# L1-distance attention scores in a vision tower: tiles 9/5/2 over VectorE, GpSimd and TensorE in place of 11/5

## The chip, the cores and the metric

One core of one Trainium2 chip runs the whole kernel in one launch. The metric is the device time of that launch in microseconds (us), lower is better. Before the change it is 2816.99 us, the median of 3 runs.

## The reference, cut to what matters

A tower runs over 128 images of 64 tokens with 64 features: wavelet tokeniser, linear attention, a mixture of experts, then the L1-distance attention that is changed here, and a routed MLP. The stage that matters:

```
q, vf, vb = split(x @ wqv_w.T + wqv_b)            # 8 heads of width w = 64 each
k = x[:, :, None, :] * wk
a[b,s,t,h] = -sum_w |q[b,s,h,w] - k[b,t,h,w]| / sqrt(64)
a = softmax over s, with one more row of zeros
o = (sum_s a[b,s,d,h] vf[b,s,h,:] + sum_s a[b,d,s,h] vb[b,s,h,:]) summed over h
y = (o * sigmoid(1.702 o)) @ fanin_w.T + fanin_b
```

For each image there are 64 x 64 x 8 = 32,768 sums of 64 absolute differences, 2.1 million differences. That is the bulk of the stage.

## The kernel before, in words

The stage loops over 64 pairs of images. Keys and queries are split into two f16 parts each. The DMAs of `fill_blocks` lay them out in `blocks`, so that one f16 matmul with a 0/1/-1 matrix `pick` makes a bank of 512 differences for each of 128 partitions: the partition is a (query, key) pair out of 128, and the column is (head, w). A tile is two such matmuls, into two banks of PSUM, 128 x 1024 differences. An image has 16 tiles.

The string `ORDER` gives the order of the 16 tiles on TensorE's in-order queue and says who sums each one:

- D: VectorE reads the tile from PSUM and sums absolute values over w in one instruction (`reduce`, L1337). Banks 0 to 3 hold two such tiles in turn, so TensorE may be two D tiles ahead of VectorE, and waits for semaphore `red` otherwise.
- A: ScalarE takes absolute values into SBUF (`absolute`, L977), and GpSimd adds the five A tiles of an image up in a tree of halvings (`batch`, L1452, and L1456 for the last step). Banks 4 and 5 hold one A tile, so TensorE waits for `abs` of the tile before. The SBUF tiles `absd0` and `absd1` alternate from image to image.

Before, ORDER has 11 D and 5 A. The work that surrounds the scores is hung between the tiles: `extra(b, k)` issues it on TensorE after tile k of image b of a pair. These are the projections of the next pair (`turn` L662, `queries` L668, `keys` L672), the values of the last (`values_b` L679, `values_f` L686), the attention sums of the pair before (`turn_attn` L694, `attend` L710 and L715) and the end of the one before that (`turn_y` L721, `fan_in` L725). On ScalarE the same is written out by hand in `pair` (L1007 to L1036): copies out of PSUM, the split of q and k (L956, L960), and eight exponentials in two parts (L989) sit between the calls of `absolute`. VectorE's `pair` (L1341) puts the low parts of q and k (`low`, L1316), `reciprocals`, `finish` and `gated` between its reduces. GpSimd has `normalise` (L1463) between two batches. The queue of SyncE issues 16 DMAs of `fill_blocks` (L388), 16 of `spread` (L397) and one load for each pair.

Of the kernel before, what the change touches and what calls it, by code (L numbers as in the profile page):

```python
# [22 lines left out]
D = 64  # L23
# [11 lines left out]

ORDER = "DADDADDADDADDADD"
ND, NA = ORDER.count("D"), ORDER.count("A")
W_SCALE = 64.0
# [71 lines left out]
def build(nc, a, out, scratch):  # L110

    with ExitStack() as ctx:
# [3 lines left out]
        def sem(name):  # L116
# [12 lines left out]
        c_rows = sb("c_rows_sb", [P, 64])  # L129
        c_cols = sb("c_cols_sb", [7, 2, 8, P])  # L130
        tok_w = sb("tok_w", [7, D])
# [13 lines left out]

        absd0 = sb("absd0", [P, NA * 1024])
        kT = absd0[:, 2048:3072].rearrange("p (b a m) -> p b a m", b=2, a=4)
        qT = absd0[:, 3072:3584]
# [95 lines left out]

        absd = [t[:].rearrange("p (n w) -> p n w", w=D) for t in (absd0, absd1)]
        wk_b = big[0:D, 0:QK].rearrange("p (h d) -> p h d", d=D)
# [18 lines left out]
            "xs", "wk_in", "consts", "xT_ps", "xT_sb", "xTq", "q_ps", "k_ps", "half", "tb0", "tb1",  # L265
            "diffD", "diffA", "red", "abs", "tree", "pooled", "spread0", "spread1", "exp", "zr", "attk", "attq_ps", "attq",
            "o_ps", "tanh", "y", "yT_ps", "yT", "fan_ps", "hx", "sum", "vb_ps", "vb", "vf_ps", "vf")}
# [53 lines left out]
        def _(sp):  # L321
# [114 lines left out]
        def _(pe):  # L436
# [220 lines left out]
            def turn(p, at):  # L657

                if at >= 3:
                    pe.wait_ge(X["sum"], p - 3)  # L660
                pe.wait_ge(X["xs"], 16 * (p + 1))
                pe.transpose(ps[7][:, 0:P], xs1[:], ident[:]).then_inc(X["xT_ps"], 1)  # L662
# [60 lines left out]
            def fan_in(p):  # L723
                pe.wait_ge(X["yT"], p + 1)
                pe.matmul(ps[7][:, 192:256], yT[:], fan[:], start=True, stop=True).then_inc(X["fan_ps"], 1)  # L725

            def image(q, b, at, extra):

# [3 lines left out]
                for k, path in enumerate(ORDER):  # L732
                    if path == "D":
                        if not (at == 0 and b == 0 and d < 2):
                            pe.wait_ge(X["red"], ND * s + d - 1)
                        unit, bank, done = 2 * d, 2 * ((b + d) % 2), "diffD"
                        d += 1
                    else:
                        if not (at == 0 and b == 0 and u == 0):
                            pe.wait_ge(X["abs"], NA * s + u)  # L740
                        unit, bank, done = 2 * (ND + u), 4, "diffA"
                        u += 1
                    for n in range(2):
                        mm = pe.matmul(ps[bank + n], pick[:, unit % 8 + n, :], blocks[:, b, unit // 16, unit // 8 % 2, :],  # L744
# [4 lines left out]
            def pair(q, odd, at):  # L749
                def extra(b, k):  # L750
                    if b == 0:
# [6 lines left out]
                        if k == 4 and at >= 3:  # L758
                            fan_in(q - 3)
                        if k == 7:  # L760
                            turn(q + 1, at)
                        if k == 9:
                            queries(q + 1, at)
                        if k == 14:
                            keys(q + 1, 1 - odd)
                    else:
                        if at >= 2:
                            if k == 4:
                                turn_attn(q - 2)
                            if 7 <= k < 10:  # L770
                                attend(q - 2, odd, k - 7)

# [14 lines left out]
            values_f(last, 1)  # L787
            fan_in(last - 2)
            for p, odd in ((last - 1, 0), (last, 1)):
                pe.wait_ge(X["attk"], p + 1)  # L790
# [45 lines left out]
        def _(act):  # L836
            act.dma_start(c_cols[:].rearrange("p a b c -> p (a b c)"), a["c_cols"]).then_inc(tok_in, 16)
            act.dma_start(tok_w[:], a["L0_tok_W"]).then_inc(tok_in, 16)
# [133 lines left out]
            def absolute(s, odd, u, first):  # L972

                act.wait_ge(X["diffA"], NA * s + u + 1)
                if u == 0 and not first:
                    act.wait_ge(X["pooled"], s - 1)
                nc.scalar.activation(absd[odd][:, 16 * u:16 * u + 16, :], pp[:, 4:6, :].rearrange("p n (h w) -> p (n h) w", w=D),  # L977
                                     ACT.Abs).then_inc(X["abs"], 1)

# [27 lines left out]
            def pair(q, odd, at):  # L1007
# [7 lines left out]
                if at >= 1:  # L1015
                    values_f(q - 1, 1 - odd)
                absolute(s, 0, 2, first)
                prepare_x(q + 1, 1 - odd)
                absolute(s, 0, 3, first)
                high_q(q + 1, False)  # L1020
                absolute(s, 0, 4, first)
                s += 1
                high_k(q + 1)
                absolute(s, 1, 0, first)
                absolute(s, 1, 1, first)
                if at >= 2:
                    turned_attn(q - 2)
                absolute(s, 1, 2, first)
                absolute(s, 1, 3, first)
                if at >= 2:  # L1030
                    gate_o(q - 2)
                if at >= 1:
                    exponentials(q - 1, 0, at == 1)
                absolute(s, 1, 4, first)
                if at >= 1:
                    exponentials(q - 1, 1, at == 1)  # L1036

            act.wait_ge(pads, PADS)
# [10 lines left out]
            turned_y(last - 2)  # L1049
            values_f(last, 1)  # L1050
            for p in (last - 1, last):
                turned_attn(p)
# [23 lines left out]
        def _(dve):  # L1076
# [10 lines left out]
            for t in (xT4[D:D + 1, :], xT1[D:D + 1], xTq[D:D + 1, :], yT[D:D + 1, :]):  # L1087
                dve.memset(t, 1.0).then_inc(pads, 1)
            dve.memset(wk_bd[:], 0.0)
            dve.memset(wqv_bd[:], 0.0)  # L1090
# [243 lines left out]
            def reduce(s, odd, b, d):  # L1334
                dve.wait_ge(X["diffD"], ND * s + d + 1)
                bank = 2 * ((b + d) % 2)
                dve.tensor_reduce(score[:, odd, b, 16 * d:16 * d + 16],  # L1337
# [3 lines left out]
            def pair(q, odd, slot, at):  # L1341
                for b in range(2):
# [3 lines left out]
                    for d in range(ND):  # L1346
                        reduce(2 * q + b, odd, b, d)
                        if b == 0 and d == 0 and at >= 2:
                            reciprocals(q - 2)
                        if b == 0 and d == 4 and at >= 3:  # L1350
                            finish(q - 3, slot)
                        if b == 0 and d == 8:
                            low(q + 1, 0)
                        if b == 1 and d == 1:
                            low(q + 1, 1)
                        if b == 1 and d == 8 and at >= 2:
                            gated(q - 2)
# [49 lines left out]
        def _(pool):  # L1407
# [37 lines left out]
            def batch(s, p, odd, b, at):  # L1445

                x = absd[b]
                pool.wait_ge(X["abs"], NA * (s + 1))
                for m, w in enumerate((32, 16, 8, 4, 2)):
# [4 lines left out]
                if at >= 2:  # L1454
                    pool.wait_ge(X[f"spread{b}"], 16 * 8 * (p - 1))
                nc.gpsimd.tensor_tensor(score[:, odd, b, 16 * ND:256].unsqueeze(2), x[:, :, 0:1], x[:, :, 1:2],  # L1456
                                        ALU.add).then_inc(X["pooled"], 1)
# [64 lines left out]
```

## Time and profile before

| what | value |
|---|---|
| runs | 2816.99 us median (2815.43 to 2818.05) |
| profiled execution | 2817.37 us, its span 2815.6 us |
| busy | VectorE 82%, TensorE 76%, GpSimd 62%, ScalarE 49% of the span |
| the attention stage | from about 700 to 2620 us of the span; granted TensorE clock 1.00 in it |

Busy time of TensorE counts each matmul until its last result is written, so neighbours overlap. A line of the timeline gives the start, the length, the engine, the source line, the operation, its output and inputs and how many instructions are merged; in brackets is the idle time of the engine before it and what ended that. Times of TensorE's weight loads stand apart, as PEld.

### The profile page before, as it was taken

To read this page: it belongs to the slowest core of one execution; us is meant where nothing else is said; L and a number is where in the kernel's file an instruction comes from. 1 tells how busy PE (TensorE), PEld (TensorE's weight loads), DVE (VectorE), ACT (ScalarE), POOL (GpSimd) and SP (SyncE) were. 2 spreads that over 40 slices of the span, in tenths; PEclk is the share of its full clock that TensorE was granted. 3 is DMA by queue.
4 is the path that set the end of the run, shared out by engine and by line. 5 is a ranking of instruction groups with operands and counts; after the bars stand their busy time and mean duration, and the time that the engine had idled before them with its cause. 6 is when DMAs were issued, how large, how long until landed. Compare 5 with 4: busy or idle time off the path is not lost.

```text
span 2815.6 us, 43219 instructions
## 1 busy us (share of the span) xinstructions
PE 2145.3 (76%) x11861; PEld 898.4 (32%) x11861; DVE 2322.0 (82%) x2847; ACT 1380.3 (49%) x2997; POOL 1750.9 (62%) x1015
## 2 busy tenths in 40 slices
PE   4649999994777777777777777777777777777466
PEld 3533333331223223223223323223222232232245
DVE  3877778788889889889899899899899899898542
ACT  0325555552455555555555555555555555555234
POOL 0103333232588888887887887887887887887411
PEclk8879999997899999999999999999999999999768
DMA  5100000000111111111111111111111111111000
GB/s 136 44 1 1 1 0 0 0 0 2 49 44 47 46 41 46 47 42 45 47 43 43 47 45 43 47 46 43 45 47 43 44 47 44 43 47 46 16 11 19
DMA packets 163208, 101.96 MB, mean 36 GB/s; under 512 B 55773, under 2 KB 161182, under 8 KB 163039
## 3 DMA queue, kind: packets, MB, share of 16 engines
q1 hardware_dynamic: 162858, 101.41, 14.6%
q8 instruction: 17, 0.28, 0.0%
q10 hardware_dynamic: 316, 0.12, 0.0%
q14 instruction: 17, 0.14, 0.0%
HBM read 10.63 MB, written 4.19 MB: 5 GB/s over the span
## 4 chain that ended last, share of the span: by engine, by line
PE 47%; DVE 29%; issue 16%; ACT 3%; DVEq 2%; DMA 1%; SPq 1%; POOL 1%; ACTq 0%; POOLq 0%
DVE score L1337 21%; PE pp L744 14%; PE pp L593 5%; DVE qk L1316 3%; PE pp L715 3%; PE pp L686 2%; PE pp L614 2%; PE pp L672 2%; PE pp L618 2%; PE pp L615 2%; PE pp L619 2%; PE pp L679 2%; PE pp L585 1%; PE pp L710 1%; ACT vb L966 1%
## 5 line engine op out<-in xcount | busy, mean ns | idle before, releaser
L1337 DVE TENSOR_REDUCE score<-pp 128x16 f32<-128x1024 f32 x1408 | 1644.1, 1217 | 192.5 <-PE pp L744 189.4
L1452 POOL TENSOR_TENSOR absd<-absd 128x2560 f32<-128x2560 f32 (+4 forms) x640 | 1450.1, 2266 | 368.0 <-ACT absd L977 327.9
L744 PE MATMUL pp<-blocks,pick 128*128 128x512 f16 x4096 | 1111.6, 382 | 199.5 <-DVE score L1337 161.8
L977 ACT ACTIVATE absd<-pp 128x1024 f32<-128x1024 f32 x640 | 655.0, 1023 | 712.7 <-PE pp L744 712.7
L744 PEld LDWEIGHTS pp<-blocks,pick 128*128 128x128 f16 x4096 | 316.2, 98 | 852.3 <-DVE score L1337 464.1
L1428 POOL TENSOR_TENSOR absd<-absd,yw 128x512 f32<-128x512 f32 x112 | 142.3, 1270 | 318.9 <-DVE yw L1255 318.9
L916 ACT ACTIVATE absd<-pp 128x512 f32<-128x512 f32 x256 | 150.8, 596 | 148.2 <-PE pp L615 145.7
L1271 DVE SCALAR_TENSOR_TENSOR absd<-pp,absd 128x512 f32<-128x512 f32 x256 | 172.4, 687 | 53.2 <-ACT absd L916 38.6
L989 ACT ACTIVATE expd<-attn 128x65 f32<-128x65 f32 x512 | 155.6, 315 | 0.0
L593 PE MATMUL pp<-absd 128*64 128x512 f32 x512 | 138.1, 618 | 0.0
L672 PE MATMUL pp<-wk_diag,xT 96*128 96x512 f32 x130 | 74.1, 652 | 73.0 <-DVE qk L1316 73.0
L662 PE MATMUL pp<-ident,xs 128*128 128x128 f32 x65 | 21.0, 323 | 128.8 <-DVE h L1332 93.7
L686 PE MATMUL pp<-wqv,xT 96*64 96x256 f32 x512 | 69.4, 392 | 44.3 <-ACT vb L966 44.3
L989 ACT ACTIVATION_READ_ACCUMULATOR expd<-attn 128x1 f32 x512 | 100.9, 197 | 0.0
L960 ACT ACTIVATE qk<-pp 128x512 f16<-128x512 f32 x65 | 38.8, 597 | 125.6 <-PE pp L672 125.6
L614 PE MATMUL pp<-x,absd 128*128 128x512 f16 x256 | 98.4, 384 | 0.8
L618 PE MATMUL pp<-x,absd 128*128 128x512 f16 x256 | 97.8, 382 | 0.3
L619 PE MATMUL pp<-x,absd 128*128 128x512 f16 x256 | 97.5, 381 | 0.0
L615 PE MATMUL pp<-x,absd 128*128 128x512 f16 x256 | 97.5, 381 | 0.0
L1316 DVE SCALAR_TENSOR_TENSOR qk<-qk,pp 128x512 f16<-128x512 f16 x130 | 88.0, 677 | 6.9 <-ACT qk L956 4.1
L1255 DVE TENSOR_TENSOR yw<-pp,absd 128x512 f32<-128x512 f32 x112 | 77.1, 688 | 17.8 <-PE pp L593 15.3
L920 ACT COPY absd<-pp 128x512 f32<-128x512 f32 x128 | 75.0, 586 | 27.7 <-PE pp L585 18.8
(200 smaller groups left out, 2201.8 us busy)
## 6 DMA issues: line engine op xcount, KB each, us to landing
blocks<-qk SPq DMA_DIRECT2D x1032, 64.0 KB, 2.0
attn<-score SPq DMA_DIRECT2D x1024, 16.0 KB, 1.8
xs<-xn SPq DMA_DIRECT2D x66, 32.0 KB, 1.8
big<-in_wrb_t SPq DMA_DIRECT2D x1, 2064.0 KB
big<-in_x_rows SPq DMA_DIRECT2D x4, 512.0 KB, 6.2
token_rows<-big SPq DMA_DIRECT2D x8, 256.0 KB, 2.0
big<-in_L_ffn_w SPq DMA_DIRECT2D x4, 512.0 KB, 10.0
out<-big SPq DMA_DIRECT2D x16, 128.0 KB, 2.0
```

The source lines that it names most:

```text
L593: mm = pe.matmul(ps[4 + k % 2][64 * e:64 * e + 64, :], w3[:, 2 * k + e, :], hid[:, 2 * (k % 2) + e, :], start=True, stop=True)
L614: pe.matmul(ps[e], w12_hi[:, 0, 2 * k + e, :], x2[:, b, :], start=True, stop=False)
L615: pe.matmul(ps[e], w12_lo[:, 0, 2 * k + e, :], x2[:, b, :], start=False, stop=True).then_inc(C["h1_ps"], 1)
L618: pe.matmul(ps[2 + e], w12_hi[:, 1, 2 * k + e, :], x2[:, b, :], start=True, stop=False)
L619: pe.matmul(ps[2 + e], w12_lo[:, 1, 2 * k + e, :], x2[:, b, :], start=False, stop=True).then_inc(C["h2_ps"], 1)
L744: mm = pe.matmul(ps[bank + n], pick[:, unit % 8 + n, :], blocks[:, b, unit // 16, unit // 8 % 2, :], start=True, stop=True)
L977: nc.scalar.activation(absd[odd][:, 16 * u:16 * u + 16, :], pp[:, 4:6, :].rearrange("p n (h w) -> p (n h) w", w=D), ACT.Abs).then_inc(X["a ...
L989: op = nc.scalar.activation(expd[:, n, :], attn[:, :, n], ACT.Exp, scale=-(float(D) ** -0.5), accum_out=zst[:, 0, n:n + 1])
L1271: dve.scalar_tensor_tensor(out=hid[:, 2 * (k % 2) + e, :], in0=ps[2 + e], scalar=1.0 / W_SCALE, in1=silu[:, e, :], op0=ALU.mult, op1=ALU.m ...
L1316: dve.scalar_tensor_tensor(out=qk[:, kind, 1, :], in0=qk[:, kind, 0, :], scalar=-LO_SCALE, in1=ps[6], op0=ALU.mult, op1=ALU.add).then_inc( ...
L1337: dve.tensor_reduce(score[:, odd, b, 16 * d:16 * d + 16], pp[:, bank:bank + 2, :].rearrange("p n (h w) -> p (n h) w", w=D), AX.X, ALU.add, ...
L1452: nc.gpsimd.tensor_tensor(x[:, :, 0:w], x[:, :, 0:w], x[:, :, w:2 * w], ALU.add).then_inc(X["tree"], 1)
```

## The change

ORDER becomes `DADDADADADDADEDE`: 9 D tiles, 5 A tiles, and 2 tiles of a new kind E. For an E tile the operands of the matmul change places: a slice of `blocks` of 128 columns is the stationary operand and `pick` is the moving one. So a bank has (two heads, w) over its 128 partitions and 512 (query, key) pairs over its columns. ScalarE takes absolute values into `abse`, a part of the same SBUF tiles, and TensorE sums over the partitions: `sum_e` uses each 128 x 128 slice of `abse` as stationary operand against `pair_ones`, two columns of ones for the two heads, all in f32. That is 16 such matmuls an image, in four groups g of four, and 32 columns of PSUM bank 7 as result, which ScalarE copies into `score` (`take_e`).

A and E tiles are now handed over by halves of 512 columns: `diffA` and `abs` count halves, and `absolute` issues two activations for each tile, so that banks 4 and 5 are used as two buffers. The items between the tiles move to other places in ORDER. `fill_blocks` waits for `diffA` in place of `diffD`, and `spread` waits for `etaken` too. The diff, cut:

```diff
-ORDER = "DADDADDADDADDADD"
-ND, NA = ORDER.count("D"), ORDER.count("A")
+ORDER = "DADDADADADDADEDE"
+ND, NP, NE = ORDER.count("D"), ORDER.count("A"), ORDER.count("E")
+NA = NP + NE
...
+        pair_ones = sb("pair_ones", [P, 2])
...
+        abse = [t[:, NP * 1024:NA * 1024].rearrange("p (m n) -> p m n", m=4) for t in (absd0, absd1)]
...
             def fill_blocks(p, b, first):
                 if not first:
-                    sp.wait_ge(X["diffD"], ND * (2 * (p - 1) + b + 1))
+                    sp.wait_ge(X["diffA"], 2 * NA * (2 * (p - 1) + b + 1))
...
             def spread(p, odd, b, first):
                 sp.wait_ge(X["pooled"], 2 * p + b + 1)
+                sp.wait_ge(X["etaken"], 2 * p + b + 1)
...
             def attend(p, odd, part):
                 if part == 0:
+                    pe.wait_ge(X["etaken"], 2 * p + 5)
...
+            def sum_e(s, b, g, first):
+                if g == 0:
+                    pe.wait_ge(X["abs"], 2 * NA * s + 2 * NA)
+                    if not first:
+                        pe.wait_ge(X["etaken"], s)
+                for m in range(4):
+                    mm = pe.matmul(ps[7][:, 384 + 8 * g + 2 * m:384 + 8 * g + 2 * m + 2], abse[b][:, m, P * g:P * g + P],
+                                   pair_ones[:], start=True, stop=True)
+                if g == 3:
+                    mm.then_inc(X["e_ps"], 1)
...
+                        for n in range(2):
+                            if not (at == 0 and b == 0 and u == 0):
+                                pe.wait_ge(X["abs"], 2 * NA * s + 2 * u + n - 1)
+                            if path == "A":
+                                unit = 2 * (ND + u) + n
+                                pe.matmul(ps[4 + n], pick[:, unit % 8, :], blocks[:, b, unit // 16, unit // 8 % 2, :],
+                                          start=True, stop=True).then_inc(X["diffA"], 1)
+                            else:
+                                m = 2 * (u - NP) + n
+                                pe.matmul(ps[4 + n], blocks[:, b, 1, 1, P * m:P * m + P],
+                                          pick[:, 4:8, :].rearrange("p a b -> p (a b)"), start=True, stop=True).then_inc(X["diffA"], 1)
...
-                        if k == 7:
+                        if k == 8:
                             turn(q + 1, at)
-                        if k == 9:
+                        if k == 10:
                             queries(q + 1, at)
-                        if k == 14:
+                        if 11 <= k < 15 and at >= 1:
+                            sum_e(2 * q - 1, 1, k - 11, False)
+                        if k == 15:
                             keys(q + 1, 1 - odd)
                     else:
+                        if 2 <= k < 6:
+                            sum_e(2 * q, 0, k - 2, at == 0)
                         if at >= 2:
-                            if k == 4:
+                            if k == 6:
                                 turn_attn(q - 2)
-                            if 7 <= k < 10:
-                                attend(q - 2, odd, k - 7)
+                            if 8 <= k < 11:
+                                attend(q - 2, odd, k - 8)
...
+            def take_e(s, p, odd, b, at):
+                act.wait_ge(X["e_ps"], s + 1)
+                if at >= 2:
+                    act.wait_ge(X[f"spread{b}"], 16 * 8 * (p - 1))
+                nc.scalar.copy(score[:, odd, b, 224:256], ps[7][:, 384:416]).then_inc(X["etaken"], 1)
```

The new order on ScalarE is, in image 0 of a pair: A0, values_b, turned_y, A1, values_f, A2, A3, prepare_x, A4, high_q, E5, take_e of the image before, E6; in image 1: high_k, A0, A1, take_e of image 0, A2, turned_attn, A3, A4, gate_o, exponentials part 0, E5, exponentials part 1, E6. On VectorE, `finish` follows reduce 3 (was 4) and `low` reduce 7 of image 0 and 2 of image 1 (were 8 and 1).

## Rows read from the trace of the kernel before

**Rows 1.** The page's head: span, and busy time of each engine.

```profile
span 2815.6 us, 43219 instructions
PE 2145.3 (76%) x11861; PEld 898.4 (32%) x11861; DVE 2322.0 (82%) x2847; ACT 1380.3 (49%) x2997; POOL 1750.9 (62%) x1015
```

**Rows 2.** Stretches: us, busy of PE, PEld, DVE, ACT, POOL, PEclk, DMA.

```profile
180.00:200.00 20.00, 1.87 (x8) 1.38 (x8) 16.51 (x11) 1.65 (x4) 0.80 (x2) 0.50 0.00 0
...
860.00:2605.00 1745.00, 1338.20 (x7795) 521.25 (x7793) 1569.84 (x1571) 925.12 (x2093) 1414.00 (x756) 1.00 0.18 45
...
2640.00:2660.00 20.00, 10.60 (x110) 8.29 (x110) 2.81 (x6) 5.85 (x23) 1.89 (x2) 0.50 0.03 7
```

**Rows 3.** Timeline of VectorE (DVE) in one pair.

```profile
2006.66 0.21 DVE L1332 TENSOR_TENSOR h<-pp,h 128x64 f32 x1
...
2007.80 4.62 DVE L1337 TENSOR_REDUCE score<-pp 128x16 f32<-128x1024 f32 x4 [0.93 <-PE pp L744]
2012.33 0.68 DVE L1316 SCALAR_TENSOR_TENSOR qk<-qk,pp 128x512 f16<-128x512 f16 x1
...
2036.67 0.21 DVE L1332 TENSOR_TENSOR h<-pp,h 128x64 f32 x1
```

**Rows 4.** Timeline of GpSimd (POOL) in the same pair.

```profile
2009.73 1.04 POOL L1463 TENSOR_TENSOR attk<-expd,zst 128x512 f32<-128x512 f32 x1
2012.38 11.66 POOL L1452 TENSOR_TENSOR absd<-absd 128x2560 f32<-128x2560 f32 x5 [1.61 <-ACT absd L977]
2024.21 0.32 POOL L1456 TENSOR_TENSOR score<-absd 128x80 f32<-128x80 f32 x1 [0.16 <-POOL absd L1452]
```

**Rows 5.** Timeline of TensorE (PE) in the same stretch.

```profile
2007.17 1.03 PE L744 MATMUL pp<-blocks,pick 128*128 128x512 f16 x4
2008.03 1.02 PE L668 MATMUL pp<-wqv,xTq 96*128 96x512 f32 x2
2008.89 1.03 PE L744 MATMUL pp<-blocks,pick 128*128 128x512 f16 x4
...
2018.80 0.66 PE L694 MATMUL pp<-ident,attk 128*128 128x128 f32 x4 [0.69 <-DVE qk L1316]
...
2032.13 1.08 PE L686 MATMUL pp<-wqv,xT 96*64 96x256 f32 x8 [0.70 <-ACT vb L966]
2033.15 0.60 PE L744 MATMUL pp<-blocks,pick 128*128 128x512 f16 x2
2033.59 0.33 PE L725 MATMUL pp<-fan,yT 96*128 96x64 f32 x2
2033.76 1.72 PE L744 MATMUL pp<-blocks,pick 128*128 128x512 f16 x6
```

**Rows 6.** The chain of work that ended last, in order of time.

```profile
2021.59 0.54 PE pp L744 x2
2022.12 0.61 PE pp L715 x16
```

**Rows 7.** Timeline of TensorE in the mixture of experts.

```profile
199.22 1.89 PE L565 MATMUL pp<-gate,xT 96*128 96x16 f32 x8 [0.67 <-ACT xT L900]
...
443.62 1.07 PE L565 MATMUL pp<-gate,xT 96*128 96x16 f32 x8
444.54 1.08 PE L603 MATMUL pp<-eye,absd 128*128 128x64 f32 x8
445.46 0.38 PE L614 MATMUL pp<-x,absd 128*128 128x512 f16 x1
```

**Rows 8.** Timeline of ScalarE (ACT) in the same pair.

```profile
2025.48 0.32 ACT L989 ACTIVATE expd<-attn 128x65 f32<-128x65 f32 x1
...
2026.69 1.02 ACT L977 ACTIVATE absd<-pp 128x1024 f32<-128x1024 f32 x1
...
2031.50 0.58 ACT L966 COPY vb<-pp 128x512 f32<-128x512 f32 x1
```

**Rows 9.** Groups by line, 900 to 2600 us: busy, mean ns; idle before.

```profile
L956 ACT ACTIVATE qk<-pp 128x512 f16<-128x512 f32 x57 | 33.7, 591 | 0.0
```

More of the change, by code:

```diff
@@ L146, in build @@
         absd0 = sb("absd0", [P, NA * 1024])
+        c_cols = absd0[0:7, 0:2048].rearrange("p (o c m) -> p o c m", o=2, c=8)
         kT = absd0[:, 2048:3072].rearrange("p (b a m) -> p b a m", b=2, a=4)
@@ L243, in build @@
         tok_rows = big[:].rearrange("p (u n) -> p u n", u=8)
-        absd = [t[:].rearrange("p (n w) -> p n w", w=D) for t in (absd0, absd1)]
+        absd = [t[:, 0:NP * 1024].rearrange("p (n w) -> p n w", w=D) for t in (absd0, absd1)]
+        abse = [t[:, NP * 1024:NA * 1024].rearrange("p (m n) -> p m n", m=4) for t in (absd0, absd1)]
         wk_b = big[0:D, 0:QK].rearrange("p (h d) -> p h d", d=D)
@@ L735, in image @@
                             pe.wait_ge(X["red"], ND * s + d - 1)
-                        unit, bank, done = 2 * d, 2 * ((b + d) % 2), "diffD"
+                        unit, bank, done = 2 * d, 2 * ((ND * b + d) % 2), "diffD"
                         d += 1
                     else:
-                        if not (at == 0 and b == 0 and u == 0):
-                            pe.wait_ge(X["abs"], NA * s + u)
-                        unit, bank, done = 2 * (ND + u), 4, "diffA"
+                        for n in range(2):
[9 more added lines that the diff above has]
+                                          pick[:, 4:8, :].rearrange("p a b -> p (a b)"), start=True, stop=True).then_inc(X["diffA"], 1)
                         u += 1
+                        extra(b, k)
+                        continue
                     for n in range(2):
@@ L788, in _ @@
             fan_in(last - 2)
+            pe.wait_ge(X["sum"], last - 1)
+            for g in range(4):
+                sum_e(2 * last + 1, 1, g, False)
+            pe.wait_ge(X["etaken"], 2 * PAIRS)
             for p, odd in ((last - 1, 0), (last, 1)):
@@ L836, in _ @@
         def _(act):
-            act.dma_start(c_cols[:].rearrange("p a b c -> p (a b c)"), a["c_cols"]).then_inc(tok_in, 16)
+            act.dma_start(c_cols.rearrange("p a b c -> p (a b c)"), a["c_cols"]).then_inc(tok_in, 16)
             act.dma_start(tok_w[:], a["L0_tok_W"]).then_inc(tok_in, 16)
@@ L972, in absolute @@
             def absolute(s, odd, u, first):
[L974 to L978, printed above, removed]
+                for n in range(2):
+                    act.wait_ge(X["diffA"], 2 * NA * s + 2 * u + n + 1)
+                    if u == 0 and n == 0 and not first:
+                        act.wait_ge(X["pooled"], s - 1)
+                    if u == NP and n == 0 and not first:
+                        act.wait_ge(X["e_ps"], s - 1)
+                    if u < NP:
+                        nc.scalar.activation(absd[odd][:, 16 * u + 8 * n:16 * u + 8 * n + 8, :],
+                                             ps[4 + n].rearrange("p (h w) -> p h w", w=D), ACT.Abs).then_inc(X["abs"], 1)
+                    else:
+                        nc.scalar.activation(abse[odd][:, 2 * (u - NP) + n, :], ps[4 + n], ACT.Abs).then_inc(X["abs"], 1)
+            def take_e(s, p, odd, b, at):
[3 more added lines that the diff above has]
+                nc.scalar.copy(score[:, odd, b, 224:256], ps[7][:, 384:416]).then_inc(X["etaken"], 1)
             def exponentials(p, part, first):
@@ L1017, in pair @@
                 absolute(s, 0, 2, first)
+                absolute(s, 0, 3, first)
                 prepare_x(q + 1, 1 - odd)
-                absolute(s, 0, 3, first)
+                absolute(s, 0, 4, first)
                 high_q(q + 1, False)
-                absolute(s, 0, 4, first)
+                absolute(s, 0, 5, first)
+                if at >= 1:
+                    take_e(s - 1, q - 1, 1 - odd, 1, at - 1)
+                absolute(s, 0, 6, first)
                 s += 1
@@ L1025, in pair @@
                 absolute(s, 1, 1, first)
+                take_e(s - 1, q, odd, 0, at)
+                absolute(s, 1, 2, first)
                 if at >= 2:
                     turned_attn(q - 2)
-                absolute(s, 1, 2, first)
                 absolute(s, 1, 3, first)
+                absolute(s, 1, 4, first)
                 if at >= 2:
@@ L1033, in pair @@
                     exponentials(q - 1, 0, at == 1)
-                absolute(s, 1, 4, first)
+                absolute(s, 1, 5, first)
                 if at >= 1:
                     exponentials(q - 1, 1, at == 1)
+                absolute(s, 1, 6, first)
             act.wait_ge(pads, PADS)
@@ L1050, in _ @@
             values_f(last, 1)
+            take_e(2 * last + 1, last, 1, 1, 4)
             for p in (last - 1, last):
@@ L1088, in _ @@
                 dve.memset(t, 1.0).then_inc(pads, 1)
+            for half in range(2):
+                for n in range(2):
+                    dve.memset(pair_ones[64 * half:64 * half + 64, n:n + 1], float(n == half))
             dve.memset(wk_bd[:], 0.0)
@@ L1349, in pair @@
                             reciprocals(q - 2)
[L1350 removed]
+                        if b == 0 and d == 3 and at >= 3:
                             finish(q - 3, slot)
[L1352 removed]
+                        if b == 0 and d == 7:
                             low(q + 1, 0)
[L1354 removed]
+                        if b == 1 and d == 2:
                             low(q + 1, 1)
[L1356 removed]
+                        if b == 1 and d == 7 and at >= 2:
                             gated(q - 2)
```

12 lines of the change are left out of this document (7 added, 5 removed).

## Prediction

> **What bounds the kernel now.** I read the page's head first, then the busy time by stretch, then one pair of images on each engine's timeline. VectorE is the busiest engine [rows 1]. In the attention stage it is busy 1569.84 of 1745 us, or 90%, against TensorE 77%, GpSimd 81% and ScalarE 53%, at a granted clock of 1.00 [rows 2]. The same instruction (`finish`) starts at 2006.66 and 2036.67, so a pair takes 30.01 us [rows 3]. Four reduces in a row take 4.62 us, 1.15 each. VectorE's own work in a pair is 22 x 1.15 + 2 x 0.6 (`low`, whose 0.68 overlaps its neighbour by 0.08) + 0.5 of small items = 27.0 us, and the other 3.0 us are waits for TensorE. So VectorE bounds the stage, with TensorE's in-order stream as the thing that it waits for. GpSimd needs, for a pair, two batches from 2012.38 to 2024.53 (12.15 us) and one 1.04 us = 25.3 us [rows 4].
>
> **TensorE's own work in a pair, now.** This must be known without its waits, from starts of neighbours [rows 5]. Four f16 matmuls of 512 columns go from 2007.17 to 2008.03: 0.215 each, 0.43 a tile, 32 tiles = 13.8. A 96 x 512 f32 projection goes from 2008.03 to 2008.89: 0.86, three of them = 2.6. `values_f` is 2032.13 to 2033.15 = 1.02; `fan_in` 2033.59 to 2033.76 = 0.17; `turn_attn` 0.66 less the drain of 0.17 = 0.49; `turn` and `turn_y` about 0.26 by the same reckoning. The three parts of `attend` cost (0.54 - 0.43) + 0.61 = 0.72 each [rows 6] = 2.2. The sum is 20.5 us of 30.
>
> **The change part by part.**
>
> VectorE loses 4 reduces a pair: 4 x 1.15 = 4.6, so it needs 22.4 us. GpSimd keeps 5 tiles and its 25.3 us. The tiles' own matmuls stay 64: an E tile streams 512 f16 columns as an A tile does.
>
> The sums of E are new. Each image has 16 f32 matmuls with 128 stationary columns and 2 moving ones. An f32 matmul shows as two instructions (`fan_in` is x2), so a group g of four is 8 instructions. The trace has nearly the same thing: eight with 128 stationary and 16 moving columns start at 443.62, the next eight with 64 moving ones at 444.54, and what follows at 445.46 [rows 7]. So a group costs 0.92 whether 16 or 64 columns stream, and 2 will not make it cheaper: the weight loads set it. `fan_in`, behind a long f16 matmul, took 0.17 for two, which suggests that the first load is hidden there. That bounds a group by 0.84 and 0.92; I take 0.88, nearest to both. Eight groups a pair are 7.0 us (6.7 to 7.4), and TensorE's own work becomes 27.5 us. That is above every other engine.
>
> The Trainium skill, "TensorE: Matmul & The Clock Gate", section "Part 2: What happens when you issue a matmul", says that the queue pulls the load of the next weights ahead, so that they load while this tile's matmul runs. If that hid these loads, a group would cost only the page's floor of about 25 ns a matmul (section "Back-to-back issue gap" calls it the issue floor), 0.2 us by an estimate from it, and the change would win. The equal 0.92 of 16 and 64 columns [rows 7] speaks against it: two columns are too short to hide a load behind.
>
> ScalarE's 10 tiles of 1.02 become 28 halves. A 512-column activation takes 0.59 [rows 9], 0.49 when the next overlaps it by 0.1, as the tile at 2026.69 and its neighbours do [rows 8]. Hence 13.7 for 9.2, plus 2 x 0.2 for `take_e`: about 21 us of work. That is not the bound, but TensorE can run just one tile of A or E ahead of it. Four exponentials take from 2025.48 to 2026.69 = 1.21 us [rows 8].
>
> Setup (four small memsets, the shared space of `c_cols`) I cost at nothing: the memsets are behind the wait for the first input, and if they were not, they would be under 1 us.
>
> SyncE issues 33 DMAs a pair as before. `spread` of the second image now waits for `take_e`, which runs in the next pair's image 0, and it lands some 6 us after image 1 begins. The exponentials come 12 us after. So this is hidden, with 6 us to spare. `fill_blocks` waits for the last E matmul, and the next image's start is 5 us or more behind its landing.
>
> **A walk through one pair.** I follow TensorE's queue with these costs. Latencies: 0.05 from ScalarE (2031.50 + 0.58 to 2032.13), the same from VectorE, 0.04 to ScalarE, a half's result 0.38 after its start (0.60 for a tile, less 0.215). Its waits for ScalarE:
> - Image 0, k1: the halves of E6 of the image before are behind the second exponentials: 0.2 + 0.3.
> - k3: `values_f` waits for the copy of `vb`, which is queued behind A0: 0.4.
> - k6: A2 waits for A1, whose halves ScalarE clears every 0.49 while TensorE makes one in 0.215: 0.3. k8, with the copy of `vf` in between: 0.6. `queries` behind `prepare_x`: 0.2.
> - Image 1: `attend` waits for the copy of the turned attention: 0.3. k13 (E5) waits for A4: 0.5. k15 (E6) waits for E5, which on ScalarE stands behind four exponentials of 1.21: 1.2 + 0.3.
>
> They sum to 2.0 and 2.2. Image 0 has 14.4 us of work (16 tiles 6.9, three projections 2.6, `values_f` 1.0, four groups 3.5, small items 0.4) and takes 16.4; image 1 has 13.0 (6.9, 3.5, `turn_attn` 0.5, `attend` 2.1) and takes 15.1. The period is 31.5 us against 30.0. VectorE is never late in it: the banks of D tiles are always free, since TensorE takes 31.5/18 = 1.75 us for each D. GpSimd has both absd tiles in time, because batch s - 2 ends before A0 of image s.
>
> 62 pairs in the steady state x 1.54 = 95 us. At the end of the stage the last batch of GpSimd starts with A4 at tile 11, not 13, which hides the last sums; I leave it at 0. On the profiled 2817.37 us this gives 2912; the median of runs, 2816.99, is as good as the same, and I predict **2912 us**. What a measurement here can tell from no change is about 0.2%, or 6 us.
>
> **Rivals.**
>
> - *Faster: the waits vanish.* TensorE has 27.5 us of work, so if less than 2.5 us of waits remain it wins. With 1.3 us of waits the period is 28.8: 2817 - 62 x 1.2 = 2743. For it: VectorE, who made TensorE wait in the old order, is out of the way. Against: six of the waits are ScalarE clearing two halves at 0.49, and do not depend on VectorE. It decides at 2.5 us. 10%.
> - *Faster: the loads are hidden*, by the page's rule. A group of 8 then costs about 0.3, as 16 instructions of 64 stationary columns take 0.61 [rows 6]; 8 x 0.58 = 4.6 us less, period 27: 2817 - 185 = 2632. It decides at 0.69 a group. [rows 7] say 0.92. 3%.
> - *The change does what it says*, VectorE's 4.6 us in full: 25.4, GpSimd's floor, 2532. It would need TensorE's stream to fit in 25.4, and it does not. Under 1%.
> - *No change:* the period comes out within 0.1 us of 30.0. Only by accident: 3%.
> - *Slower still: the clock.* Between the four groups TensorE streams only 0.43 us of every 1.31. In [rows 2] the clock stood at 0.50 for 2640 to 2660 though TensorE was busy 10.6 of 20 us with small f32 matmuls; the attention stage itself held 1.00 with `attend` in it. If the clock fell from 2.4 to 1.2 GHz for both stretches of groups, a group costs 1.89 (the eight at 199.22, at a clock of 0.50 [rows 2, 7]) and a tile 0.86: 4 x (1.01 + 0.43) = 5.8 us a stretch, 11.5 a pair, up to 3620 us. The skill's same page, "A second HAM failure mode: psum-queue depth-cycling", warns that short idles between groups of matmuls can make the clock oscillate. Only a part of the stretches seems possible to me. 6%.
> - *Slower by more waits:* each new handover on TensorE costs a little that my walk leaves out. This is in the likeliest case's range.
>
> **How the numbers follow.** The likeliest case has 78%. Its own range: a group at 0.84 or 0.92 moves the period by -0.3 or +0.3, the waits by a quarter of 4.2 either way, so 30.2 to 32.9, or 2829 to 2995. I set the low end at 2830, the high end at 2995. Below lie about 13% in the faster cases and above the clock's 6%. Faster by over 0.2% 14%, within 3%, slower 83%.
>
> **What would show it.** After the change VectorE's share falls to about 70% in the stage and TensorE's rises to 90% or over. The distance of two `finish` is 31.5. The `sum_e` groups take 0.84 to 0.92 each, 7 us a pair. TensorE's largest waits are for `absolute` on ScalarE, the longest, over 1 us, before the E6 tile of image 1. GpSimd idles 5 to 6 us a pair. The prediction is wrong if a group costs under 0.7, if TensorE waits less than 2.5 us a pair, or if the clock leaves 1.00.

## The result, and the profile after

The changed kernel takes 2975.19 us (median of 4 runs), the kernel before 2817.52 us on the same chip. The ratio is 1.056, with a 95% interval of 1.054 to 1.058: 158 us slower. The forecast was 2912 us with 2830 to 2995 us as range. The trace shown is of the execution of 2975.75 us. The string ORDER above has two tiles the wrong way round: the changed kernel and all its variants run `DADADDADADDADEDE`, with the second A as tile 3 and not 4. The counts are the same.

First the page's head: span, busy times, and the granted clock in 40 slices.

```profile
span 2974.0 us, 54804 instructions
...
PE 2594.0 (87%) x15957; PEld 1437.0 (48%) x15957; DVE 2063.8 (69%) x2595; ACT 1692.5 (57%) x4277; POOL 1754.2 (59%) x1015
...
PEclk8879999996899999999999999999999999999768
```

Beside [rows 1], VectorE falls from 82% to 69% and TensorE rises from 76% to 87%. The busiest engine has changed. Next the stretches, read as [rows 2]:

```profile
760.00:900.00 140.00, 129.22 (x782) 74.63 (x781) 95.75 (x95) 86.80 (x227) 102.12 (x57) 0.92 0.18 42
900.00:2700.00 1800.00, 1653.33 (x10998) 954.63 (x10998) 1276.46 (x1280) 1155.70 (x3121) 1350.04 (x719) 0.97 0.17 42
```

In the attention stage TensorE is busy 92% of the time, VectorE 71%, ScalarE 64%, GpSimd 75%. The clock is 0.97 where it was 1.00, a small figure that will matter. VectorE's timeline gives the length of pairs, as in [rows 3]; `gated` is issued once a pair:

```profile
2007.88 0.21 DVE L1393 SCALAR_TENSOR_TENSOR osb<-osb,pp 128x64 f32<-128x64 f32 x1
...
2041.22 0.21 DVE L1393 SCALAR_TENSOR_TENSOR osb<-osb,pp 128x64 f32<-128x64 f32 x1
...
2072.71 0.21 DVE L1393 SCALAR_TENSOR_TENSOR osb<-osb,pp 128x64 f32<-128x64 f32 x1
```

The pairs are not alike: one takes 33.34 us, the next 31.49. The mean is 32.42 against 30.01 before. TensorE's timeline shows where they part. In the first pair, image 0, tile 14 and on:

```profile
2023.05 0.95 PE L745 MATMUL pp<-pair_ones,absd 128*128 128x2 f32 x8
2023.86 0.59 PE L778 MATMUL pp<-blocks,pick 128*128 128x512 f16 x2
2024.29 1.05 PE L745 MATMUL pp<-pair_ones,absd 128*128 128x2 f32 x8
2025.20 1.01 PE L772 MATMUL pp<-pick,blocks 128*128 128x512 f16 x2
2026.01 1.91 PE L680 MATMUL pp<-wk_diag,xT 96*128 96x512 f32 x2
2027.71 0.94 PE L778 MATMUL pp<-blocks,pick 128*128 128x512 f16 x2
```

and the same place one pair later, with the E6 tile of image 1:

```profile
2057.45 0.95 PE L745 MATMUL pp<-pair_ones,absd 128*128 128x2 f32 x8
2058.26 0.59 PE L772 MATMUL pp<-pick,blocks 128*128 128x512 f16 x2
2058.69 1.02 PE L680 MATMUL pp<-wk_diag,xT 96*128 96x512 f32 x2
2059.55 0.59 PE L778 MATMUL pp<-blocks,pick 128*128 128x512 f16 x2
...
2073.86 0.88 PE L772 MATMUL pp<-pick,blocks 128*128 128x512 f16 x2 [0.97 <-ACT absd L1026]
```

The E tile, the key projection and the next D tile take 0.81, 1.70 and 0.78 us from start to start in the first, 0.43, 0.86 and 0.43 in the second. The stretches say why:

```profile
2025.00:2028.00 3.00, 3.00 (x8) 1.28 (x8) 0.71 (x1) 1.32 (x4) 2.92 (x2) 0.50 0.05 11
2056.00:2059.00 3.00, 3.00 (x23) 2.56 (x22) 2.21 (x3) 1.60 (x4) 3.00 (x1) 1.00 0.00 0
```

The clock stood at 0.50 in one, 1.00 in the other, 1.2 and 2.4 GHz, and TensorE was recorded busy all of the time in both. In both it had just worked through four groups of sums without a gap. Among these each 1.24 us (2023.05 to 2024.29) holds one tile, 0.43 us of columns, and eight matmuls of two columns each, which are nearly all weight load. Why the clock falls in one pair of two and not in the other is not shown.

The drop is not the whole of the 1.85 us between the two pairs. From start to start, the last group, the E tile, the projection and the D tile take 0.91 + 0.81 + 1.70 + 0.78 = 4.20 us in the first and 0.81 + 0.43 + 0.86 + 0.43 = 2.53 in the second: the drop costs 1.67 us. The other 0.18 us is no clock: in wide_ones below, at a clock of 1.00, the pairs still alternate, with `gated` at 1987.74, 2019.87, 2051.81 and 2083.95, which is 32.13, 31.94 and 32.14. The likely place is the loop's end, as the kernel's loop holds two pairs: the D tile behind it starts 1.07 us after the tile before (2009.02 to 2010.09), for 0.71 inside the loop (2042.37 to 2043.08), and the profile names no engine that it waited for.

### The profile page after: what moved, and what is told of

It reads as the page before. It is cut to its first block, busy times and chain, and to the rows that moved or that the text cites. A ratio compares the mean times of both kernels' runs of the same rounds, so it can differ in the third digit from the quotient of the medians.

```text
span 2974.0 us, 54804 instructions
## 1 busy us (share of the span) xinstructions
PE 2594.0 (87%) x15957; PEld 1437.0 (48%) x15957; DVE 2063.8 (69%) x2595; ACT 1692.5 (57%) x4277; POOL 1754.2 (59%) x1015
## 4 chain that ended last, share of the span: by engine, by line
PE 64%; ACT 12%; DVE 10%; issue 10%; DVEq 2%; DMA 1%; ACTq 0%; POOL 0%; SPq 0%; POOLq 0%
PE pp L745 14%; PE pp L778 12%; DVE score L1403 5%; PE pp L768 5%; PE pp L599 4%; ACT expd L1044 3%; ACT absd L1026 3%; PE pp L680 3%; PE pp L772 3%; PE pp L725 3%; PE pp L694 2%; PE pp L620 2%; PE pp L676 2%; PE pp L624 2%; ACT absd L1023 2%
## 5 line engine op out<-in xcount | busy, mean ns | idle before, releaser
L1403 DVE TENSOR_REDUCE score<-pp 128x16 f32<-128x1024 f32 x1152 | 1380.7, 1222 | 605.8 <-PE pp L778 525.0
L1023 ACT ACTIVATE absd<-pp 128x512 f32<-128x512 f32 x1280 | 696.3, 598 | 414.8 <-PE pp L768 408.9
L745 PEld LDWEIGHTS pp<-pair_ones,absd 128*128 128x128 f32 x4096 | 544.2, 194 | 75.7 <-issue 0.7
L745 PE MATMUL pp<-pair_ones,absd 128*128 128x2 f32 x4096 | 493.5, 243 | 0.3 <-DVE h L1398 0.3
L778 PEld LDWEIGHTS pp<-blocks,pick 128*128 128x128 f16 x2304 | 199.9, 110 | 261.7 <-DVE score L1403 125.1
L1026 ACT ACTIVATE absd<-pp 128x512 f32<-128x512 f32 x512 | 278.2, 600 | 64.3 <-PE pp L772 62.6
L772 PE MATMUL pp<-pick,blocks 128*128 128x512 f16 x512 | 188.3, 410 | 78.2 <-ACT absd L1026 62.9
L768 PEld LDWEIGHTS pp<-blocks,pick 128*128 128x128 f16 x1280 | 122.8, 107 | 253.3 <-ACT absd L1023 91.7
L958 ACT ACTIVATE absd<-pp 128x512 f32<-128x512 f32 x256 | 150.8, 596 | 148.0 <-PE pp L621 143.4
L1033 ACT COPY score<-pp 128x32 f32<-128x32 f32 x128 | 23.8, 186 | 244.0 <-PE pp L745 244.0
L772 PEld LDWEIGHTS pp<-pick,blocks 128*128 128x128 f16 x512 | 54.0, 123 | 179.5 <-ACT absd L1026 120.1
L1044 ACT ACTIVATION_READ_ACCUMULATOR expd<-attn 128x1 f32 x512 | 108.0, 211 | 0.0
L620 PE MATMUL pp<-x,absd 128*128 128x512 f16 x256 | 98.4, 384 | 0.6
L624 PE MATMUL pp<-x,absd 128*128 128x512 f16 x256 | 97.8, 382 | 1.0 <-DVE absd L1337 0.3
L625 PE MATMUL pp<-x,absd 128*128 128x512 f16 x256 | 97.5, 381 | 0.0
```

The source lines that it names most:

```text
L620: pe.matmul(ps[e], w12_hi[:, 0, 2 * k + e, :], x2[:, b, :], start=True, stop=False)
L745: mm = pe.matmul(ps[7][:, 384 + 8 * g + 2 * m:384 + 8 * g + 2 * m + 2], abse[b][:, m, P * g:P * g + P], pair_ones[:], start=True, stop=True)
L768: pe.matmul(ps[4 + n], pick[:, unit % 8, :], blocks[:, b, unit // 16, unit // 8 % 2, :], start=True, stop=True).then_inc(X["diffA"], 1)
L772: pe.matmul(ps[4 + n], blocks[:, b, 1, 1, P * m:P * m + P], pick[:, 4:8, :].rearrange("p a b -> p (a b)"), start=True, stop=True).then_inc ...
L1023: nc.scalar.activation(absd[odd][:, 16 * u + 8 * n:16 * u + 8 * n + 8, :], ps[4 + n].rearrange("p (h w) -> p h w", w=D), ACT.Abs).then_inc ...
L1026: nc.scalar.activation(abse[odd][:, 2 * (u - NP) + n, :], ps[4 + n], ACT.Abs).then_inc(X["abs"], 1)
```

## The experiments

Four kernels ran on one chip first, then four, then two, each set beside the kernel before (2818.01, 2817.77 and 2817.05 us).

| kernel | us | ratio to before (95%) | PEclk, 900 to 2400 us |
|---|---|---|---|
| changed kernel | 2975.19 | 1.056 (1.054 to 1.058) | 0.97 |
| no_sums | 2668.00 | 0.947 (0.945 to 0.948) | 1.00 |
| f16_sums | 2671.39 | 0.948 (0.947 to 0.950) | 1.00 |
| exps_early | 3039.27 | 1.079 (1.077 to 1.081) | 0.90 |
| keys_between | 3199.44 | 1.136 (1.134 to 1.139) | 0.88 |
| wide_ones | 2945.06 | 1.045 (1.044 to 1.047) | 1.00 |
| no_sums_in_image0 | 2823.94 | 1.002 (1.001 to 1.003) | 0.97 |
| no_sums_in_image1 | 2870.77 | 1.020 (1.018 to 1.022) | 0.97 |
| f16_exps_early | 2594.13 | 0.921 (0.920 to 0.923) | 1.00 |
| wide_exps_early | 2865.81 | 1.018 (1.016 to 1.019) | 1.00 |
| wide_whole_tiles | 3020.33 | 1.072 (1.070 to 1.074) | 1.00 |

### What the sums cost: no_sums and f16_sums

```diff
-                for m in range(4):
+                for m in (range(3, 4) if g == 3 else ()):      # no_sums
```

> Leaves out 15 of the 16 f32 sums of the E tiles in each image, so the scores of these tiles are not summed. Everything else stays. My theory (TensorE's stream bounds; the sums are work on it and their stretch also costs clock): 8 groups x 0.81 us = 6.5 us a pair go, and the stretches at 1.2 GHz with them (0.9 us a pair). GpSimd's 25.3 us is then near, and ScalarE's waits stay, so the pair takes 25.5 to 27.5 us and the run 2550 to 2680 us. Rival (ScalarE's hand-over of halves bounds, and the sums only fill TensorE's waiting time): the pair stays at 29 us or more, the run above 2760 us.

```diff
-        pair_ones = sb("pair_ones", [P, 2])
+        pair_ones = sb("pair_ones", [P, 2], F16)               # f16_sums
-        abse = [t[:, NP * 1024:NA * 1024].rearrange("p (m n) -> p m n", m=4) for t in (absd0, absd1)]
+        abse = [t[:, NP * 1024:NP * 1024 + 1024].bitcast(F16).rearrange("p (m n) -> p m n", m=4) for t in (absd0, absd1)]
```

> The absolute values of the E tiles and the columns of ones are f16, not f32; the sums have lower precision in their inputs. The count of matmuls is the same, but each is one instruction and not two, with an f16 weight load. My theory (the f32 weight loads are the price of a group, 0.81 us for 8): a group falls to 0.15 to 0.4 us, the pair loses 3.3 to 5.3 us plus what the clock gives back: 2640 to 2770 us, below the kernel before. Rival (a small matmul costs a fixed time whatever its type, and the pair is bound by ScalarE): less than 100 us are won, above 2875 us.

They took 2668.00 and 2671.39 us. So all the f32 sums, with what hangs on them, cost 307 us, and as f16 the same sums cost 3. Both runs bear out my theory against the rivals. TensorE's timeline of f16_sums:

```profile
2024.51 0.60 PE L768 MATMUL pp<-blocks,pick 128*128 128x512 f16 x2
2024.95 0.24 PE L745 MATMUL pp<-pair_ones,absd 128*128 128x2 f16 x4
2025.05 0.59 PE L778 MATMUL pp<-blocks,pick 128*128 128x512 f16 x2
...
2033.45 0.66 PE L702 MATMUL pp<-ident,attk 128*128 128x128 f32 x4 [0.64 <-DVE qk L1382]
```

A group is four instructions and takes 0.10 us, from 2024.95 to 2025.05, where the f32 group takes 0.81 (2023.05 to 2023.86). The last row shows that not all of it comes back as time. The turned attention now waits 0.64 us for `low`, for which it did not wait in the changed kernel. The period is 27.76 us, from `reciprocals` on VectorE:

```profile
2016.07 0.19 DVE L1388 RECIPROCAL zst<-zst 128x8 f32<-128x8 f32 x1
...
2071.58 0.19 DVE L1388 RECIPROCAL zst<-zst 128x8 f32<-128x8 f32 x1
```

(two pairs, 55.51 us). Two pairs of the changed kernel at full clock would take 31.49 + 31.67 (33.34 less the drop's 1.67), 31.58 on average. So this is 3.8 us less, for 8 x 0.71 = 5.7 us of work taken off TensorE. The other 1.9 us became waits.

### Where the exponentials stand: exps_early

```diff
                 absolute(s, 1, 3, first)
+                if at >= 1:
+                    exponentials(q - 1, 0, at == 1)
+                    exponentials(q - 1, 1, at == 1)
                 absolute(s, 1, 4, first)
                 if at >= 2:
                     gate_o(q - 2)
-                if at >= 1:
-                    exponentials(q - 1, 0, at == 1)
                 absolute(s, 1, 5, first)
-                if at >= 1:
-                    exponentials(q - 1, 1, at == 1)
                 absolute(s, 1, 6, first)
```

> All eight exponentials stand on ScalarE behind A3 of image 1, where it idles 2.6 us in the trace, in place of before E5 and before E6. My theory (TensorE waits for ScalarE at E6 and at the next pair's A0 because of the exponentials): these waits, about 1.5 us a pair, go: 62 x 1.5 = 93 us less, 2860 to 2910 us, if the clock's drops stay as they are. Rival (the waits only move to the next late thing, such as A1's halves or the copy of vb): less than 30 us are won, above 2945 us.

It took 3039.27 us, 64 us more than the changed kernel. My theory missed, and so did the rival: the time is above its 2945 us, but not because the waits moved. The stretches of two pairs in a row:

```profile
2078.00:2113.00 35.00, 33.71 (x194) 19.84 (x192) 21.75 (x23) 20.47 (x55) 22.86 (x14) 0.80 0.16 38
2113.00:2143.00 30.00, 28.39 (x197) 16.91 (x197) 22.48 (x24) 20.36 (x56) 23.79 (x14) 1.00 0.19 45
```

The values of the last pair, `values_b`, start here on TensorE and 30.13 us later:

```profile
2101.68 1.71 PE L745 MATMUL pp<-pair_ones,absd 128*128 128x2 f32 x8
...
2113.59 1.02 PE L687 MATMUL pp<-wqv,xT 96*128 96x512 f32 x2
...
2143.72 1.02 PE L687 MATMUL pp<-wqv,xT 96*128 96x512 f32 x2
```

So a pair at full clock is 30.13 us. The same pair of the loop, counted from `values_b` too, takes 31.32 us in the changed kernel where its clock held (974.51 to 1005.83). The move takes off 1.2 us, a little under the 1.5 forecast. (The 1.4 in an expectation below set 30.1 against the 31.49 of the loop's other pair.) The other pair has two drops, one of them in image 1, where the group at 2101.68 takes 1.56 us to the next start (2103.24) for 0.81. The move did its work and the clock took more than all of it back.

### Breaking up the four groups: keys_between

```diff
-                        if 11 <= k < 15 and at >= 1:
+                        if 11 <= k < 13 and at >= 1:
                             sum_e(2 * q - 1, 1, k - 11, False)
-                        if k == 15:
+                        if k == 13:
                             keys(q + 1, 1 - odd)
+                        if 14 <= k and at >= 1:
+                            sum_e(2 * q - 1, 1, k - 12, False)
```

On ScalarE `take_e` of the image before moves behind E6.

> The f32 projection of the keys moves from behind tile 15 to behind tile 13 of image 0, between the second and the third group of sums; groups three and four follow tiles 14 and 15; the work is the same. My theory (the granted clock falls in every second pair because four groups of sums follow each other in image 0, with the projection of the keys behind them): with the projection between them the clock holds 1.00 and 62 x 0.93 = 58 us are won: 2905 to 2935 us. Rival (the drop does not hang on this order): PEclk stays at 0.97 and the time within 15 us of 2975 us.

It took 3199.44 us, the worst of all. Both theories failed: one had a gain, the other no change. TensorE's timeline and the stretch:

```profile
2020.60 2.08 PE L680 MATMUL pp<-wk_diag,xT 96*128 96x512 f32 x2 [0.67 <-DVE qk L1384]
...
2036.90 1.71 PE L745 MATMUL pp<-pair_ones,absd 128*128 128x2 f32 x8
```

```profile
2020.00:2044.00 24.00, 23.40 (x96) 16.00 (x96) 8.49 (x8) 7.72 (x16) 10.04 (x6) 0.51 0.12 29
```

At tile 13 the projection is early: it waits 0.67 us for the low part of the queries. In this pair the clock was down for some 24 us, through both stretches of groups. A group takes 1.57 us in it, 2036.90 to the next start at 2038.47, for 0.81. A pair without a drop shows what the order itself costs: `gated` at 2048.15 and 2080.59, 32.44 us for 31.49. That is some 59 of the 224 us (62 x 0.95), and the rest is the clock. Whether the drops grew longer by the new wait or by the new order is not separated. The clock, once down among the sums, can stay down.

### Columns in place of 2: wide_ones

The suspected cause by itself: the same weight loads, the same number of matmuls, but 96 columns streamed by each.

```diff
-        pair_ones = sb("pair_ones", [P, 2])
+        pair_ones = sb("pair_ones", [P, 96])
-                    mm = pe.matmul(ps[7][:, 384 + 8 * g + 2 * m:384 + 8 * g + 2 * m + 2], abse[b][:, m, P * g:P * g + P],
+                    mm = pe.matmul(ps[7][:, 384 + 8 * g + 2 * m:384 + 8 * g + 2 * m + 96], abse[b][:, m, P * g:P * g + P],
-                    dve.memset(pair_ones[64 * half:64 * half + 64, n:n + 1], float(n == half))
+                    dve.memset(pair_ones[64 * half:64 * half + 64, n:96:2], float(n == half))
```

> As the changed kernel, but each f32 sum streams 96 columns of ones in place of 2; each writes over the surplus columns of the one before it, so the result is the same. In the expert layer a group of 8 took 0.92 us with 64 moving columns as with 16. My theory (the granted clock falls because TensorE streams next to no columns while it loads the sums' weights): a group stays at 0.8 to 1.0 us, PEclk in the stage becomes 1.00, and the time 2900 to 2940 us. Rival (the clock falls for another reason, such as the loads or the f32 type): PEclk stays at 0.97 and the time at 2965 us or more.

2945.06 us, 30 us less for more work. TensorE's timeline, then the stretch:

```profile
2065.81 1.03 PE L745 MATMUL pp<-pair_ones,absd 128*128 128x96 f32 x8
2066.67 0.59 PE L772 MATMUL pp<-pick,blocks 128*128 128x512 f16 x2
```

```profile
900.00:2400.00 1500.00, 1377.82 (x9262) 817.33 (x9263) 1074.55 (x1076) 970.24 (x2619) 1142.93 (x611) 1.00 0.19 42
```

The clock is 1.00 throughout this stretch. A group takes 0.86 us, 0.05 more than with 2 columns, or 0.4 us a pair, and the time is 5 us above my window. The f32 loads are the same and the clock holds, so the loads and the type alone don't bring it down. The 2 columns alone don't either: f16_sums has them too and held 1.00, with groups of 0.10 us. It fell where both came together, 0.81 us of f32 loads and next to no columns behind them. The clock fell only a few times in the third kernel with 96 columns, wide_whole_tiles, below. An accident of timing, a rival to this reading, would have to spare wide_ones, wide_exps_early and both f16 kernels, of 2594 to 2945 us, and hit all five kernels with f32 groups of 2 columns, of 2824 to 3199 us. It is unlikely, though no run tests it by itself.

### Which stretch brings the clock down: no_sums_in_image0 and no_sums_in_image1

```diff
-                for m in range(4):
+                for m in (range(4) if b == 0 else range(3, 4) if g == 3 else ()):   # no_sums_in_image0
+                for m in (range(4) if b == 1 else range(3, 4) if g == 3 else ()):   # no_sums_in_image1
```

> Leaves out 15 of 16 sums of the second image of each pair, the four groups that TensorE gets in image 0. Without any sums the pair was 27.7 us at a clock of 1.00, with all 31.5 us at a clock of 1.00 and 33.3 with the drop. My theory: half of the 3.8 us goes, and the drop with it, since it begins in this stretch: 62 x (1.9 + 0.9) = 175 us less, 2770 to 2830 us, PEclk 1.00. Rival (the drop comes from the groups in image 1 as well, as both stretches have the same work): PEclk 0.98 or less, 2850 us or more.

> Leaves out 15 of 16 sums of the first image of each pair, the four groups that TensorE gets in image 1. My theory: half of the 3.8 us goes and the drop in image 0 stays: 62 x 1.9 = 118 us less, 2830 to 2890 us, PEclk 0.96 to 0.98. Rival (the two stretches of sums only together bring the clock down): PEclk 1.00 and 2770 to 2820 us.

2823.94 and 2870.77 us. The second time is as my theory had it. The first is just inside its window, but by luck: the clock is 0.97 in both kernels, so my claim that the drop belongs to the stretch in image 0 is wrong. The rival of no_sums_in_image0 had that right (the groups of image 1 bring the clock down as well), with too high a time. The rival of no_sums_in_image1 is refuted: the groups of both images are not needed together, and either stretch alone is enough.

### With the clock out of the way: wide_exps_early, f16_exps_early, wide_whole_tiles

Each is a combination of edits above. The last puts the hand-over of whole tiles back, on ScalarE as shown, with TensorE waiting once for each A or E tile:

```diff
-                for n in range(2):
-                    act.wait_ge(X["diffA"], 2 * NA * s + 2 * u + n + 1)
+                act.wait_ge(X["diffA"], 2 * NA * s + 2 * u + 2)
...
+                    nc.scalar.activation(absd[odd][:, 16 * u:16 * u + 16, :],
+                                         pp[:, 4:6, :].rearrange("p n (h w) -> p (n h) w", w=D), ACT.Abs).then_inc(X["abs"], 1)
```

> The f32 sums with 96 moving columns, at which the clock held 1.00 (2945 us), and all eight exponentials behind A3 of image 1. With 2 columns the same move made the kernel 64 us slower. My theory (the move is worth 1.4 us a pair wherever the clock holds, and only the clock spoilt it): 2850 to 2875 us, PEclk 1.00. Rival (the earlier exponentials pull the clock down whatever streams, as the stream gets denser in small matmuls): PEclk under 0.98 and 2930 us or more.

> Sums in f16, and all eight exponentials behind A3 of image 1. With f32 sums the earlier exponentials made a pair without a clock drop 1.4 us shorter (30.1 for 31.5), and the drops took more than that back; with f16 sums the clock held 1.00. My theory (the clock alone spoilt the earlier exponentials): 62 x 1.0 to 1.4 us less than the 2671 us of f16 sums: 2580 to 2615 us; GpSimd's 25.3 us a pair would allow 2530 us. Rival (a shorter stream lets the clock fall here too): PEclk under 0.99 and 2660 us or more.

> The f32 sums with 96 moving columns (2945 us), and the halves of the A and E tiles undone: one activation of 1024 columns, and TensorE waits for both banks before the next A or E tile, as before the change. My theory (the halves shorten TensorE's waits for ScalarE at each A and E tile by 0.2 to 0.5 us): 1 to 2.5 us more a pair, 3005 to 3100 us. Rival (the halves cost more in added waits and instructions than they bring): under 2940 us.

All three times came as my theory had them. wide_exps_early took 2865.81 us, 79 less than wide_ones; f16_exps_early 2594.13, 77 less than f16_sums. That is 1.3 us a pair each. The same edit that made the changed kernel 64 us slower is worth nearly 80 where the clock holds. wide_whole_tiles took 3020.33 us, 75 more than wide_ones: the halves are worth 1.2 us a pair and are the good part of the change. A part of this is the clock again, for it fell here a few times even with 96 columns, as in

```profile
1703.00:1708.00 5.00, 4.61 (x11) 1.65 (x11) 1.80 (x3) 2.85 (x11) 4.92 (x2) 0.66 0.26 58
```

which the 1.00 of the table, a mean over 1500 us, does not show. So 96 columns are no guarantee. The stage of f16_exps_early:

```profile
900.00:2400.00 1500.00, 1367.66 (x9389) 611.70 (x9387) 1290.82 (x1304) 1177.30 (x3165) 1378.92 (x737) 1.00 0.21 51
```

TensorE is at 91%, GpSimd 92%, VectorE 86%, ScalarE 78%. This is the version to keep: 7.9% below the kernel before and 12.8% below the changed one. It sums absolute values that are rounded to f16, in two of 16 tiles.

## Why the prediction was right, and where it was off

**What bounds.** Right. VectorE's share fell, TensorE's rose to 92% in the stage, and its stream sets the period. GpSimd and VectorE follow it; GpSimd idles 8.1 us a pair, where 5 to 6 were forecast.

**The price of the sums.** A group was put at 0.88 us with 0.84 and 0.92 as bounds; it took 0.81, just outside. The expert layer's rows were the right ones, and a group here is 0.11 us cheaper than theirs. Against 0.88 this is 0.6 us a pair. The Trainium skill, "TensorE: Matmul & The Clock Gate", section "Part 2: What happens when you issue a matmul", says that the next tile's weights load while this tile's matmul runs. With the 25 ns of issue floor in "Back-to-back issue gap" a group would have cost 0.2 us, by an estimate from these two sections; the trace does not agree for f32 weights behind two columns. The f16 group of four took 0.10, which is four times that floor; whether its loads are hidden or only short, no run shows.

**The walk.** It gave 31.5 us for a pair at full clock and the trace has 31.49, but the agreement is partly luck, since two errors cancel. The work is smaller than forecast, 26.8 us for 27.5, as the groups are cheaper. The waits are larger, 4.7 us from start to start for 4.2 (the walk's own waits of image 1 add up to 2.3 and not 2.2). Image 0 was to take 16.4 and takes 16.5 (2043.08 to 2059.55, the first D tile of each image). But the walk said that "VectorE is never late in it", and there it was wrong:

```profile
2049.60 0.60 PE L778 MATMUL pp<-blocks,pick 128*128 128x512 f16 x2 [0.28 <-DVE score L1403]
...
2050.93 0.32 PE L670 MATMUL pp<-ident,xs 128*128 128x128 f32 x1 [0.27 <-DVE h L1398]
...
2051.99 0.61 PE L778 MATMUL pp<-blocks,pick 128*128 128x512 f16 x2 [0.30 <-DVE score L1403]
```

Two D tiles wait for VectorE's reduces and `turn` waits for `finish`, in every pair. Each costs about 0.45 us from start to start, 1.4 us together. The waits for ScalarE at tiles 6 and 8 of image 0, which the walk had in their place at 0.9 us, do not appear as such. The largest wait, before E6 of image 1, was foreseen over 1 us (1.2 + 0.3). It is 0.97 in the idle time at 2073.86, and 1.14 from start to start (2072.29 to 2073.86, less the tile's 0.43). That the exponentials cause the longest is shown by the three kernels that move them.

**What was off: the clock.** The term "at a granted clock of 1.00" was carried over from [rows 2], and the rival that the clock falls was given 6% and a time of up to 3620 us. It did come, in its small form: one drop of 1.67 us in every second pair, so 0.84 us a pair. A group at the lower clock takes 1.56 us, not the 1.89 of that rival. "If the clock leaves 1.00" was one of the prediction's three signs of being wrong, and this one came true; its other two, a group under 0.7 us and waits under 2.5 us a pair, did not (the waits are 4.7 us from start to start; in recorded idle time, 146.67 us of the 1800 above, they are 2.6). The account of the result is then 62 x (31.49 - 30.01) = 92 us from work and waits, where 95 were forecast, 62 x 0.84 = 52 from the clock, and 62 x 0.09 = 6 from the 0.18 us of every second pair that is no clock, which the walk left out. That makes 150 of 158 us. The rest most likely lies at the start of the stage, where the first `gated` comes at 808.62 us, 11.7 later than before (796.94), and the clock was 0.92 in the stretch of 760 to 900 us. So the time came inside the range with a term of over 50 us put at nothing: the margin that was meant for the waits took up the clock, and that is luck. wide_ones fits this account. It is 30 us faster though each pair has 0.45 us more (31.94 for 31.49), 28 us in all; that makes 58 us, against 52 for the steady drops and 6 at the start (its first `gated` is at 802.68). The Trainium skill ("TensorE: Matmul & The Clock Gate", "A second HAM failure mode: psum-queue depth-cycling") blames short idles between groups of matmuls. Here the trace shows no idle from 2019.28 until the clock fell at 2024.99, and the short idles before that stand in the next pair too, where the clock held. What it shows are loads with next to nothing streamed behind them.

**The rivals.** That the waits vanish did not happen: moving the exponentials took 1.3 us of them and left the rest. That the loads are hidden is refuted for f32. With the sums in f16 the loads do all but vanish, and the gain that this rival had in mind comes in part: 2671 us, not 2632. Even then VectorE's 4.6 us of relief gave only 30.01 - 27.76 = 2.25 us.

## What to carry to other kernels

Moving sums onto TensorE with the data as stationary operand was paid in weight loads here, not in columns: in f32 two instructions of 0.1 us each for every 128 x 128 block, in f16 one of 0.025. Before such a move, add up TensorE's own stream without its waits; here it was 20.5 of 30 us and looked roomy, and 6.5 more with the waits that came with it made it the bound. Read the granted clock in every experiment before its time. A true improvement (the exponentials) measured 64 us slower until the clock was held, and a TensorE that is recorded busy all the time may still run at half clock, as from 2025 to 2028 us.

## What the runs showed that I had not expected

- The clock of TensorE fell to 1.2 GHz while it was recorded busy 3.00 of 3.00 us, after four groups of f32 matmuls with 2 moving columns between f16 tiles, and held 2.4 GHz when the same matmuls had 96 columns, which cost 0.05 us a group more, or when they were f16, with 2 columns.
- From about 1050 us on it fell in every second pair alike, at the same place. The pair between did the same work and held 1.00.
- In keys_between it stayed at 0.51 on average for 24 us of TensorE being busy 23.4 us.
- A kernel with half of its sums left out (no_sums_in_image0) kept the same mean clock of 0.97 as the full one.
